# Order and banks on TensorE at four places of a one-launch vision tower with routed experts

## What is computed

```python
h  = patches(x) @ W.T + b, class token first, + pos_embedding   # 16 images, 37 tokens each, 256 features
a  = LN(h) * g1 + b1
Q, K, V = low-rank projections of a (rank 48 per head, 16 heads of 16)
h1 = h + softmax(causal(Q K^T / 4)) V @ out_U @ out_V + out_b
x2 = LN(h1) * g2 + b2
h2 = h + h1 + gelu(x2 @ fc1_U @ fc1_V + fc1_b) @ fc2_U @ fc2_V + fc2_b
h3 = LN(h2)
w, idx = top 3 of softmax(h3 @ gate_w.T) over 15 experts, weights normalised
y  = sum over idx of w * expert(h3) + shared_expert(h3)         # gated GELU, 256 wide; shared 512 wide
out = LN(h3 + y)
```

## Time and profile before

| | |
|---|---|
| median of 3 runs | 215.9 us (215.08 to 216.38) |
| the profiled execution, its own time | 215.5 us |
| its span, from first to last instruction | 213.7 us |
| busy: PE, PE's weight loads | 202.1 us (95%), 127.6 us (60%) |
| busy: DVE, ACT, POOL | 111.8 us (52%), 94.6 us (44%), 120.4 us (56%) |
| mean granted clock of PE | 0.994 of full speed |
| DMA | 38.32 MB, 179 GB/s in the mean |

### The profile page before, as it was taken

The page is one execution under the profiler, slowest core; times in us unless marked ns, Lnnn a source line. Parts: engine busy times, 40 slices in busy tenths (PEclk is TensorE's granted clock), DMA queues, the critical chain, the costliest instruction groups (busy, mean ns, idle before and its releaser), DMA issues.

```text
span 213.7 us, 4423 instructions
## 1 busy us (share of the span) xinstructions
PE 202.1 (95%) x1557; PEld 127.6 (60%) x1557; DVE 111.8 (52%) x309; ACT 94.6 (44%) x219; POOL 120.4 (56%) x148
## 2 busy tenths in 40 slices
PE   7999899989998899989999999999999999998972
PEld 4786577667786676756877773454444554454620
DVE  5665598748873445274599743733444232231044
ACT  2003634668868373562438764243323333234033
POOL 0040079849979867949999376207756661347000
PEclk9999999999999999999999999999999999999997
DMA  6999999950000299941031033219975321112592
GB/s 206 388 413 324 396 418 415 428 200 0 6 3 0 82 386 372 416 123 49 2 101 30 22 100 98 49 38 352 362 289 192 97 74 52 49 49 99 156 244 89
DMA packets 13854, 38.32 MB, mean 179 GB/s; under 512 B 2729, under 2 KB 4618, under 8 KB 13834
## 3 DMA queue, kind: packets, MB, share of 16 engines
q1 hardware_dynamic: 11818, 32.54, 41.9%
q0 software_dynamic: 2016, 5.51, 8.1%
HBM read 29.26 MB, written 4.06 MB: 156 GB/s over the span
## 4 chain that ended last, share of the span: by engine, by line
PE 82%; DVE 6%; DMA 6%; ACT 1%; issue 1%; POOL 1%; SPq 1%; POOLq 0%; DVEq 0%; ACTq 0%
PE ps L375 71%; DMA wres<-y_dram 3%; PE ps L1833 3%; PE ps L1643 2%; PE ps L1873 2%; PE ps L1656 2%; DMA embed_sb<-embed 1%; DMA y_dram<-ln_mem,dest_i 1%; PE ps L1575 1%; POOL y_dram L655 1%; DVE ln_mem L1026 1%; DVE nw_i L1010 1%; DVE nw L1015 1%; DVE nw L1016 1%; SPq L432 1%
## 5 line engine op out<-in xcount | busy, mean ns | idle before, releaser
L375 PE MATMUL ps<-wres,cT 128*64 (+1 forms) x360 | 63.1, 469 | 0.6 <-DVE cT L1399 0.6
L375 PEld LDWEIGHTS ps<-wres,cT 128*64 128x64 f32 (+1 forms) x360 | 25.3, 131 | 28.4 <-issue 21.2
L655 POOL DMA_INDIRECT y_dram<-ln_mem,dest_i x21 | 20.6, 982 | 26.7 <-ACT ln_mem L862 23.4
L418 POOL TENSOR_TENSOR wres<-wres,fac_mem 128x512 f32<-128x512 f32 x22 | 27.2, 1273 | 2.9 <-DVE ln_rs L1017 2.9
L646 POOL DMA_INDIRECT embed_sb<-x_dram,gather_i x21 | 20.3, 967 | 12.8 <-PE ps L1833 5.0
L1392 DVE TENSOR_TENSOR fac_mem<-ps,h 128x256 f32<-128x256 f32 x21 | 8.9, 422 | 24.5 <-ACT h L856 24.5
L856 ACT ACTIVATE h<-ps 128x256 f32<-128x256 f32 x21 | 8.0, 383 | 28.5 <-PE ps L375 28.5
L375 PE MATMUL ps<-h,stage 128*128 128x296 f32 x64 | 17.9, 418 | 0.0
L1399 DVE COPY cT<-ps 128x256 f32<-128x256 f32 x21 | 8.8, 424 | 16.3 <-PE ps L375 14.7
L862 ACT ACTIVATE ln_mem<-ps 128x256 f32<-128x256 f32 x21 | 8.0, 383 | 16.4 <-PE ps L375 16.4
L375 PEld LDWEIGHTS ps<-h,stage 128*128 128x128 f32 x64 | 11.8, 190 | 3.8 <-issue 0.4
(11 more groups left out here) (211 smaller groups left out, 383.9 us busy)
## 6 DMA issues: line engine op xcount, KB each, us to landing
wres<-experts SPq DMA_DIRECT2D x15, 768.0 KB, 13.9
fac_mem<-experts SPq DMA_DIRECT2D x11, 256.0 KB, 8.0
wres<-ut SPq DMA_DIRECT2D x3, 768.0 KB, 8.8
embed_sb<-embed SPq DMA_DIRECT2D x5, 416.0 KB, 5.6
stage<-shared SPq DMA_DIRECT2D x2, 771.0 KB, 16.8
wres<-y_dram SPq DMA_DIRECT2D x4, 384.0 KB, 5.4
stage<-wres SPq DMA_DIRECT2D x2, 512.0 KB, 3.5
f1v<-fc_v SPq DMA_DIRECT2D x1, 512.0 KB
```

Of the source, the lines that this page charges most:

```text
L375: return nc.tensor.matmul(o, w, x, start=start, stop=stop)
L418: nc.gpsimd.tensor_tensor(w1(e, c), w1(e, c), row, ALU.subtract).then_inc(less_done, 1)
L655: pool.indirect_dma_start(out=y_dram[:, :], out_offset=bass.IndirectOffsetOnAxis(ap=dest_i[:, column(i):column(i) + 1], axis=0), in_=ys[:, ...
```

## The change

At four places:

1. **Composing.** PE runs compose(2) ahead of spread(ln1, 1), and DVE copies it out ahead of the second scaling.
2. **Banks.** The projections of half 1 get other banks: Q in 6 and 7, K in 4 and 5, V in 6 and 7. The product for `z_b` goes to the last column of bank 3. It waits for the second subtraction of maxima (`s_cen`) and no more for K and V being out of their banks; those waits move to the first turn's transposes (K), its value transposes (V) and the products of turn 1 (V). Pair 3's scores, which write bank 3, wait for `z_b`.
3. **Last tile.** The transposes of the last tile's gated rows come ahead of second(18), not after second(19).
4. **Newton steps.** The three steps of one tensor and a number (shift, half, guess) take their number from a tensor of one column, repeated along the row: two tensors each. POOL's two waits before its last portions go. DVE fills three small constants at its start. The semaphore `route_init` is named `const_init` and counts them too.

```diff
+        nw_one = sb("nw_one", [P, 1], I32)
+        nw_half = sb("nw_half", [P, 1])
+        nw_magic = sb("nw_magic", [P, 1])
...
-        PROJ_BANK = (4, 5, 6, 7, 0, 1, 4, 5, 6, 7, 4, 5)
+        PROJ_BANK = (4, 5, 6, 7, 0, 1, 6, 7, 4, 5, 6, 7)
+        ZB_COL = 511
...
                 less_first(pool, e)
-            pool.wait_ge(ln2.rs, 2)
             sums(1)
             for e in range(LESS_TO[1], LESS_TO[2]):
                 less_first(pool, e)
-            pool.wait_ge(ln3.rs, 1)
             for e in range(LESS_TO[2], LESS_TO[3]):
...
-            nc.scalar.activation(z_b[:, :], ps[:, 7, 0:1], ACT.Copy).then_inc(cmp_done, 1)
+            nc.scalar.activation(z_b[:, :], ps[:, 3, ZB_COL:ZB_COL + 1], ACT.Copy).then_inc(cmp_done, 1)
...
             nc.vector.memset(eps_t[:, :], EPS).then_inc(init_done, 1)
+            nc.vector.memset(nw_one[:, :], 1).then_inc(const_init, 1)
+            nc.vector.memset(nw_half[:, :], -0.5).then_inc(const_init, 1)
+            nc.vector.memset(nw_magic[:, :], float(0x5f3759df)).then_inc(const_init, 1)
...
                 step(nc.vector.tensor_scalar(t, var, EPS, None, ALU.add))
-                step(nc.vector.tensor_scalar(nw_i[:, :], t.bitcast(I32), 1, None, ALU.arith_shift_right))
-                nc.vector.tensor_scalar(nw[:, 0], t, -0.5, None, ALU.mult).then_inc(nw_done, 1)
+                dve.wait_ge(const_init, 5)
+                step(nc.vector.tensor_tensor(nw_i[:, :], t.bitcast(I32), nw_one[:, :].to_broadcast([P, QT]),
+                                             ALU.arith_shift_right))
+                nc.vector.tensor_tensor(nw[:, 0], t, nw_half[:, :].to_broadcast([P, QT]), ALU.mult).then_inc(nw_done, 1)
                 next(steps)
-                step(nc.vector.tensor_scalar(y.bitcast(I32), nw_i[:, :], -1.0, float(0x5f3759df), ALU.mult, ALU.add))
+                step(nc.vector.scalar_tensor_tensor(y.bitcast(I32), nw_i[:, :], -1.0, nw_magic[:, :].to_broadcast([P, QT]),
+                                                    ALU.mult, ALU.add))
...
             inverse_std(ln1, 1)
+            composed_out(2)
             scale(ln1, 1, xc[:, 1])
-            composed_out(2)
...
             weight_transposed(1)
+            compose(2)
             spread(ln1, 1)
-            compose(2)
...
                 if g in (6, 7):
-                    pe.wait_ge(q_done, g - 5)
+                    pe.wait_ge(k_done, g - 5)
                 if g in (8, 9):
-                    pe.wait_ge(k_done, g - 7)
+                    pe.wait_ge(q_done, g - 7)
...
-            pe.wait_ge(vt_done, 4)
-            pe.wait_ge(k_done, 4)
+            pe.wait_ge(s_cen, 2)
             pe.wait_ge(ld_mlp, 96)
             for c in range(DC):
-                last = mm(ps[:, 7, 0:1], f1u[:, c], vec[:, C_LN2B + c:C_LN2B + c + 1], c == 0, c == DC - 1)
+                last = mm(ps[:, 3, ZB_COL:ZB_COL + 1], f1u[:, c], vec[:, C_LN2B + c:C_LN2B + c + 1], c == 0, c == DC - 1)
...
                 if p == 0:
-                    pe.wait_ge(cmp_done, 5)
+                    pe.wait_ge(vt_done, 4)
...
                 pe.wait_ge(s_exp, p + 1)
+                if p == 0:
+                    pe.wait_ge(k_done, 4)
...
                 pe.wait_ge(v_staged, p * 4 + 4)
+                if p == 0:
+                    pe.wait_ge(vt_done, 3)
...
                 last.then_inc(v_mm, 1)
+                if p == 1:
+                    pe.wait_ge(cmp_done, 5)
...
+            gated_transposed(NT - 1)
             second(NT - 3)
             second(NT - 2)
-            gated_transposed(NT - 1)
             second(NT - 1)
```

More of the change, by code:

```diff
@@ L344, in vit_tower_kernel @@
             sem(n) for n in ("mask_done", "pos_mm", "comb_done", "route", "hot_done", "pick_done"))
-        rt_init = sem("route_init")
+        const_init = sem("const_init")
         own_done, tab_mm, tab_out, idx_done = sem("own_done"), sem("tab_mm"), sem("tab_out"), sem("idx_done")
@@ L921, in _ @@
             nc.vector.memset(zrow[:, :], 0.0).then_inc(init_done, 1)
-            nc.vector.memset(low_bits[:, :], TM - 1).then_inc(rt_init, 1)
-            nc.vector.memset(tm_t[:, :], float(TM)).then_inc(rt_init, 1)
+            nc.vector.memset(low_bits[:, :], TM - 1).then_inc(const_init, 1)
+            nc.vector.memset(tm_t[:, :], float(TM)).then_inc(const_init, 1)
             for k in range(1, KP):
@@ L1282, in choose @@
                                         ALU.add).then_inc(rt, 1)
-                dve.wait_ge(rt_init, 2)
+                dve.wait_ge(const_init, 5)
                 dve.wait_ge(rt, 16)
```

## The result

The changed kernel takes 225.6 us in the median of 6 runs (225.2 to 226.0), beside 215.7 us for the kernel before: a ratio of 1.045, 95% interval 1.041 to 1.049. The forecast was 226.6. The profiled execution took 225.2 us with a span of 223.4 (before 215.5 and 213.7), so its span is 9.7 us longer.

What follows compares the result with a forecast made beforehand. PE was taken as the bound, busy 95% of the span, so its waits counted. On the profiled 215.5 us, -0.1 - 0.6 - 0 + 9.4 + 2.0 + 0 = +10.7 gave 226.2, median 226.6 us, range 220 to 232.

Steps and rivals of the forecast that it cites:

- Composing: PE before the second spreading: 0.87 us gap closes, but scores(0, 0) waits for POOL's keys; gain 0.1 us, bounds 0 and 0.9.
- Banks: PE before the product for `z_b`: the 0.60 us wait for ACT goes; gain 0.6 us, bounds 0 and 0.9.
- Last tile: Last tile's copy: 0.6 us wait closes, POOL's scatters stay at 1.27 us; gain 0, bounds 0.4 lost and 0.6 gained.
- First chain: DVE's first Newton chain: nine steps held by POOL at 1.30 us spacing, three free, ending at 91.0: +9.4 us.
- Low clock: After the first chain: PE, idle some 9 us, returns at half speed for some 4 us: +2.0, between 0 and 4.
- Second chain: DVE's second Newton chain: one step waits as now, the others meet POOL's scalings: 0, bounds -1 and +2.5 us.
- The sum: All terms for the whole kernel: +10.7 us, 226.2 for the profiled execution and 226.6 as a median.
- The mechanism as it was put: Newton steps with two SBUF inputs contend with POOL's subtractions; DVE gets in once per POOL operation, at its end.
- Rival 1: Newton chains: two-tensor steps aren't held beside POOL, so only the removed waits matter; median 214.5 us; chance 8%.
- Rival 2: First Newton chain: DVE, once it has the port, holds off POOL for the rest; median 216.7 us; chance 7%.
- Rival 3: Second Newton chain: POOL's scalings hold eleven steps for their whole length; +7, 233.6 us; chance 3%.

Runs made afterwards that it cites:

- experiment 4: The changed kernel with 68 fill products on PE ahead of spread(ln2, 1), keeping PE busy while DVE's first chain is held: 1.057 of the kernel before.
- experiment 1: The changed kernel with POOL's two waits put back and the rewritten Newton steps kept: 0.9935 of the kernel before, 214.7 us beside 216.6.
- Experiment 2: The kernel before with only POOL's two waits taken out, three Newton steps keeping one tensor and a number: 1.051, 227.3 us beside 216.6.
- experiment 3: The changed kernel with each 128x512 subtraction on POOL split into two of 128x256: 1.052 of the kernel before.
- experiment 9: The kernel before with composing, banks and last tile changed, POOL's two waits out, every Newton step having an operand in PSUM: 0.9937.

## Why the prediction was right, and where its terms were off

*Composing, -0.1, bounds 0 to 0.9; here it was about -0.6.* The path is as said: PE has no idle time before the spreading (25.02), and scores(0, 0) waits for keys, 0.33 us. But the prediction said "still at 37 us", and the row says 36.36. The keys follow the landing of the first experts, which came at 27.16 and not 27.93. Without the edit PE would have come at 36.9 (an estimate: 14.95 us after its first spreading at 21.98, as in the kernel before), so the earlier landing let 0.6 of the 0.9 us through. The prediction took this landing as fixed, as the edit doesn't touch it. It differs between executions: 27.16, 28.17 and 28.95 in the changed kernel and in experiments 4 and 1, whose programs are the same up to there. Alone, the edit's gain is within -0.2 to +1.1 us.

*Banks, -0.6.* The 0.60 us wait is gone, and the edit alone gave 0.7.

*Last tile, 0.* The wait is gone, the scatters still leave one each 1.27 us (203.06, 204.34, 205.61, 206.89), and alone it gave nothing measurable.

*First chain, +9.4; it was +8.6.* The count was right: nine steps held, the first by the sum and eight by the subtractions, then POOL's stall on the bias row of expert 10, then three free. Two sizes were off. The spacing was taken from DVE's key blocks, 1.30 us, and is 1.23, that of POOL's own operations (9.86 / 8): 0.6 us over eight steps. And the last held step gets in at once when POOL stalls, where 0.25 us had been allowed.

*Low clock, +2.0; it was +2.4*, shown by experiment 4: with PE kept busy the stretch takes the 9.8 us it took before. The size came partly by luck. PE ran slowly for some 6 us (88.64 to about 94.6), not 4, and half speed over 6 us would be 3.0; and the 454 ns products at the start of the run, from which the 4 us were taken, stand where this view reads a granted clock of 1.00.

*Second chain, 0; it was +0.5.* One step is held as said, for 1.02 us. Not counted were the starts of scalings, at which four steps take 0.39 to 0.45, the duration L1260 had shown.

*The sum.* It came to +10.7, and the span shows +9.7. The three terms of the fourth place were off by -0.8, +0.4 and +0.5, which nearly cancel: that the total fits so well is luck. The rest lies ahead of the first chain, which starts 1.6 us earlier where 0.7 was forecast: 0.5 more by the composing, 0.2 more by the banks, 0.2 by an earlier start of this execution. The medians lie 9.9 us apart.

*The mechanism as it was put* has one wrong part. The prediction had steps held because of two SBUF inputs, nine of the twelve before, and took the rewriting of the other three as part of the cost. Experiment 2 shows the one-tensor steps held just as long; L1010 at 91.73 had one input too, and was a hint that this reason is too narrow. It didn't change the number, since in the changed kernel all twelve have two. What makes the loss is the removal of two lines on POOL, and, as far as experiments 1 and 2 can tell, nothing on DVE.

*Rival 1*, steps not held, is refuted by the first row beside a subtraction, 77.99. *Rival 2*, DVE keeps its turn: refuted, POOL's eight operations take 9.86 us (9.88 before), and DVE gets one step in for each. *Rival 3*, the full length of a scaling: refuted by the steps of 0.22 to 0.25 us beside the scalings, from 102.51 on. The Trainium skill, "SBUF — State Buffer", section "Who interferes with whom", has the second of two contending instructions blocked fully. For subtractions the trace agrees (steps of 1.19 us beside operations of 1.23); for scalings it doesn't: a step that meets one loses about 0.2 of its 0.92 us.

*The expectations of experiments 3 and 4* missed their totals although their mechanism held. Both priced the first chain and the clock by themselves, and left the second chain where it was. It moved against POOL's subtractions, whose time is set by a DMA landing and by how many operations they are, and not by PE.

What stays open. First, the key operation of 1.36 us on POOL at 47.24, which the prediction put down to DVE holding POOL off. It comes again at the turns that follow: in the changed kernel two key blocks take 1.75 us together at 45.20 and 1.73 at 48.30, where two take 0.82 elsewhere. DVE has two key blocks of its own inside the long one each time (0.53 us for both at 47.78 in the kernel before), and these are hardly held (four take 0.97 with POOL idle). So here POOL is the one that waits; what gives DVE the turn wasn't tried. Second, the two waits were always taken out and put back together. Third, every step of experiment 9 reads something from PSUM; whether writing there alone would do isn't shown.

## What to carry to other kernels

A chain of small dependent operations on DVE in SBUF loses one POOL operation per step while POOL streams two SBUF tensors: count the steps times POOL's operation, not DVE's busy time, and look at what keeps the two apart (here two semaphore waits that no data needed) before it is taken away. If they must overlap, let each DVE step read one operand from PSUM. And when a gain moves one engine against another whose times stand still, redo the sum at the next place where the two meet: with a shorter first chain and with a warm clock the second chain came dearer, by 2.1 and 2.8 us.

## What was not expected of the hardware

- A held DVE step doesn't slow POOL: eight subtractions take 9.86 us with eight steps held beside them, 9.89 with none held, 9.88 in the kernel before.
- A 128x74 step on DVE of one tensor and a number, from SBUF to SBUF, is held by POOL's 128x512 subtraction: 1.20 and 1.32 us (experiment 2) for steps of 0.20 and 0.19 alone.
- The price is one POOL subtraction for each step, whatever its size: 1.19 us beside 1.23, 0.65 beside 0.68 (experiment 3).
- POOL's scaling, one tensor and a number, holds a DVE step by about 0.2 us and only at its start: 0.39 to 0.45 us, otherwise 0.22 to 0.25.
- Steps that read an operand from PSUM are not held at all, whether the other input and the output are in SBUF or not: 0.22 to 0.24 us (experiment 9).
